# Softmax denominators in four column tiles, and one addition moved behind two maxima

## What is computed

```python
q = (layernorm(x) @ Wq).reshape(B, Nq, h, dh)        # 1 x 2048 x 16 x 64
k = (context @ Wk).reshape(B, Nk, h, dh)             # 1 x 1601 x 16 x 64
v = (context @ Wv).reshape(B, Nk, h, dh)
scores = einsum('bqhd,bkhd->bhqk', q, k) * scale
attn = softmax(scores, axis=-1)                      # exp(s - max) / sum
out = einsum('bhqk,bkhd->bqhd', attn, v) @ Wo + bo
x = x + out                                          # then the experts
```

## Time and profile before

| | us |
|---|---|
| median of three runs | 1381.43 |
| the profiled execution | 1375.65 |
| its span, first to last instruction | 1373.9 |
| TensorE matmuls busy | 1296.3 (94%) |
| VectorE busy | 1023.0 (74%) |
| GpSimd busy | 906.8 (66%) |
| ScalarE busy | 798.8 (58%) |

### The profile page before, as it was taken

The page is one execution under the profiler, slowest core; times in us unless marked ns, Lnnn a source line. Parts: engine busy times, 40 slices in busy tenths (PEclk is TensorE's granted clock), DMA queues, the critical chain, the costliest instruction groups (busy, mean ns, idle before and its releaser), DMA issues. The chain is left out here.

```text
span 1373.9 us, 24841 instructions
## 1 busy us (share of the span) xinstructions
PE 1296.3 (94%) x8308; PEld 819.1 (60%) x8308; DVE 1023.0 (74%) x1708; ACT 798.8 (58%) x1061; POOL 906.8 (66%) x464
## 2 busy tenths in 40 slices
PE   7989999999999999999999999999999926999996
PEld 5655555555555555554555555555447915999996
DVE  5867877887787788778778877887977775666662
ACT  5456666666665666566566666656664213657753
POOL 3347877887787688779777877977687002445553
PEclk9999999999999999999999999999999956999998
DMA  9530010002001100200010010002313442545422
GB/s 275 201 111 9 25 42 31 17 20 62 17 25 39 37 17 16 65 17 17 26 57 16 17 57 25 17 17 77 128 39 123 160 151 60 146 130 126 106 37 28
DMA packets 76631, 88.83 MB, mean 65 GB/s; under 512 B 11579, under 2 KB 56412, under 8 KB 76508
## 3 DMA queue, kind: packets, MB, share of 16 engines
q1 hardware_dynamic: 69724, 78.32, 17.5%
q0 software_dynamic: 6784, 8.94, 4.0%
HBM read 58.98 MB, written 27.99 MB: 63 GB/s over the span
## 5 line engine op out<-in xcount | busy, mean ns | idle before, releaser
L915 POOL TENSOR_TENSOR acc_p<-acc_p,x_in 128x1024 f32<-128x1024 f32 x192 | 488.0, 2542 | 135.5 <-ACT x_in L1012 128.7
L112 DVE TENSOR_REDUCE mx_part<-ps_m 128x1 f32<-128x512 f32 x552 | 363.0, 685 | 173.5 <-PE ps_m L81 172.7
L1012 ACT ACTIVATE x_in<-ps_s 128x1024 f32<-128x1024 f32 x384 | 380.6, 1024 | 100.7 <-PE ps_s L831 71.3
L843 PE MATMUL ps_o<-x_in,v 128*64 128x512 f32 x1664 | 406.2, 606 | 0.0
L820 PE MATMUL ps_s<-q,k 64*128 64x512 f32 x2496 | 386.4, 396 | 1.2 <-ACT x_in L1012 1.2
L820 PEld LDWEIGHTS ps_s<-q,k 64*128 64x128 f32 x2496 | 273.8, 185 | 41.5 <-ACT x_in L1012 7.8
L81 PE MATMUL ps_m<-k,q 64*128 64x512 f32 x736 | 215.6, 456 | 9.8 <-PEq L228 3.8
L843 PEld LDWEIGHTS ps_o<-x_in,v 128*64 128x64 f32 x1664 | 99.5, 136 | 180.7 <-issue 140.7
L81 PEld LDWEIGHTS ps_m<-k,q 64*128 64x128 f32 x736 | 100.9, 184 | 168.3 <-issue 112.5
L915 DVE TENSOR_TENSOR acc_d<-acc_d,x_in 128x1024 f32<-128x1024 f32 x96 | 166.4, 1733 | 5.2 <-ACT x_in L1012 4.9
L697 ACT ACTIVATE kept<-ps_m 128x512 f32<-128x512 f32 x184 | 109.7, 596 | 83.0 <-PE ps_m L81 82.9
(11 more groups left out here) (251 smaller groups left out, 1936.3 us busy)
## 6 DMA issues: line engine op xcount, KB each, us to landing
w_in<-in_w SPq DMA_DIRECT2D x16, 1024.0 KB, 5.7
v_st<-rec_scr SPq DMA_DIRECT2D x64, 128.0 KB, 2.9
o_scr<-v_st SPq DMA_DIRECT2D x32, 256.0 KB, 2.1
v<-v_scr SPq DMA_DIRECT2D x8, 832.0 KB, 5.2
v_scr<-c_in SPq DMA_DIRECT2D x10, 512.0 KB, 3.9
c<-o_scr SPq DMA_DIRECT2D x2, 1792.0 KB, 8.0
x_in<-in_x SPq DMA_DIRECT2D x4, 512.0 KB, 9.8
m_rows<-mx_t SPq DMA_DIRECT2D x128, 1.0 KB
```

The source lines that it names most:

```text
L112: dve.tensor_reduce(part[:, j // S.MF, j % S.MF:j % S.MF + 1], bank[:, 0:S.MC], AX.X, ALU.max).then_inc(done or G.rough_used[hd], 1)
L843: last = pe.matmul(ps_o[hd * HP:hd * HP + DH, :], v[b][:, s, hd * DH:(hd + 1) * DH], probs[:, g % RING, hd * QC:(hd + 1) * QC], start=(s = ...
L915: eng.tensor_tensor(acc, other, probs[:, (u * KT + t) % RING, :], ALU.add).then_inc(done, 1)
L1012: act.activation(probs[:, g % RING, :], ps_s[:, g % 2, :], ACT.Exp, bias=G.pad_bias[:, 0:1] if s == KT - 1 else 0.0, scale=SCALE).then_inc ...
```

## The change

The denominators are computed in four column tiles instead of two: each matmul takes 32 columns of ones and 256 columns of sums and writes 32 partitions. ScalarE copies 256 columns instead of 512, and one DMA moves the four rows in place of two that move a row each. In VectorE's order the addition of tiles 2 and 3 stands behind the two maxima of slot 4.

```diff
+DEN_TILES = 4
...
+    DP, DQ = P // DEN_TILES, UQ // DEN_TILES
...
         def pe_den(pe, u, unit, bank=None):
             pe.wait_ge(joined, unit + 1)
-            for b in range(2):
-                last = pe.matmul((ps_x if bank is None else bank)[b * HP:(b + 1) * HP, :], G.ones[:, 0:HP], acc_p[:, u % 2, b * QC:(b + 1) * QC],
-                                 start=True, stop=True)
+            for i in range(DEN_TILES):
+                last = pe.matmul((ps_x if bank is None else bank)[i * DP:(i + 1) * DP, 0:DQ], G.ones[:, 0:DP],
+                                 acc_p[:, u % 2, i * DQ:(i + 1) * DQ], start=True, stop=True)
             last.then_inc(den_ready, 1)
...
-            wait_for(act, den_moved, 32 * unit)
-            act.activation(den_sb[:], (ps_x if bank is None else bank)[:], ACT.Copy).then_inc(den_copied, 1)
+            wait_for(act, den_moved, 16 * unit)
+            act.activation(den_sb[:], (ps_x if bank is None else bank)[:, 0:DQ], ACT.Copy).then_inc(den_copied, 1)
...
             sp.wait_ge(den_copied, unit + 1)
-            for b in range(2):
-                sp.dma_start(den_c[8 * b:8 * b + 8, :], den_sb[b * HP:b * HP + 1, :]).then_inc(den_moved, 16)
+            sp.dma_start(den_c[:], den_sb[0:P:DP, :]).then_inc(den_moved, 16)
...
-            dve.wait_ge(den_moved, 32 * (unit + 1))
+            dve.wait_ge(den_moved, 16 * (unit + 1))
...
                 if s == MAX_SLOT and not (last and u == UNITS - 1):
                     dve_max(dve, unit + 1)
-                if s == DVE_TILES[1] + 1:
-                    add_tile(dve, 0, u, unit, slot - s, dve=True)
                 if job:
                     j, ahead = job
                     dve_rough(dve, j, unit + ahead, (unit + ahead) * MJOBS + j)
+                if s == DVE_TILES[1] + 1:
+                    add_tile(dve, 0, u, unit, slot - s, dve=True)
...
-            G.den_sb = lasting("den_sb", [P, S.QC], F32)
+            G.den_sb = lasting("den_sb", [P, S.UQ // DEN_TILES], F32)
```

## The result

The changed kernel took 1403.90 us, the median of four runs (1401.84 to 1406.14), against 1381.40 us for the kernel before: 1.0157 times as long, with a 95% interval of 1.0144 to 1.0170. That is 22.5 us slower. The profiled execution took 1406.14 us.

The account below looks back on a forecast made before the run. TensorE was taken to bound the attention loop. 21 x 1.42 = +29.8, 7 x 0.66 = +4.6 and 3 x -0.27 = -0.8 gave +33.6 us on 1381.43: 1415.0 us, range 1398 to 1425.

Parts of the forecast that it names:

- GpSimd stands first by 0.27 us in 21 units: Attention loop: GpSimd's addition of tile 4 starts at 541.17, VectorE's moved addition only at 541.44, in 21 units.
- VectorE is kept out for the whole instruction, about 3.2 us: VectorE's addition of tiles 2 and 3 ends 1.08 us after GpSimd's; mean about 3.2 us instead of 1.22.
- VectorE is not kept out: Rival: VectorE's addition isn't blocked or comes first everywhere; 31 x -0.27 = -8.4, 1373.0 us; chance 0.11.
- The maximum of slot 5 comes 1.42 us later and TensorE waits for it: Slot 5's first maximum moves from 543.13 to 544.55; TensorE's load for slot 6's rough scores moves to 545.30.
- The unit pays all of it, +1.42: Each of 21 units lengthens by the whole shift, +1.42 us; together +29.8 us.
- nothing behind the wait has slack: TensorE bounds the attention loop, so whatever it is made to wait is lost, with nothing given back.
- My lower bound: A stalled unit costs at least +1.2 us, if a waited-for load hands over to its matmul 0.2 us faster.
- The third units are a tie, counted +0.66: Seven third units of a pair: additions tie; +1.60 us if GpSimd is first, -0.27 if VectorE; mean +0.66, sum +4.6.
- Part one saves 0.27 us where it is seen: Denominators in four column tiles on TensorE take 0.69 us against 0.96, form changes included; saves 0.27 us a unit.
- Last pair 3 x -0.27 = -0.8: Last head pair, three units: VectorE has no projection to finish, is in time, and the tiles' gain shows.
- The small edits are worth nothing: ScalarE's shorter copy of the denominators and one DMA instead of two change nothing TensorE waits for: 0.
- A sign that missed: TensorE waits for VectorE's maxima some 1.7 us in each of 21 to 28 units, 35 to 47 us in all.

Follow-up runs that it names:

- order alone: Kernel before with VectorE's addition of tiles 2 and 3 moved behind slot 4's two maxima, still two column tiles: 1409.80 us, ratio 1.0170.
- tiles alone: Changed kernel with VectorE's addition of tiles 2 and 3 put back ahead of the maxima, four column tiles kept: 1387.63 us, ratio 1.0013.
- GpSimd held, two tiles: Kernel before with VectorE's addition behind the maxima, and GpSimd's addition of tile 4 waiting for it: 1379.55 us, ratio 0.9986.
- GpSimd held, four tiles: Changed kernel with GpSimd's addition of tile 4 waiting until VectorE's addition of tiles 2 and 3 is done: 1377.67 us, ratio 0.9941.
- GpSimd's addition in two: Changed kernel with GpSimd's addition of tile 4 done as two instructions of 512 columns: 1386.24 us, ratio 1.0003.
- addition between the maxima: Changed kernel with VectorE's addition of tiles 2 and 3 placed between slot 4's two maxima: 1384.13 us, ratio 1.0023.
- more matmuls, same form: Kernel before with each denominator matmul cut into two of 256 columns, in the same two column tiles: 1382.04 us, ratio 1.0006.

## Why the prediction was right, step by step

I forecast +33.6 us and 1415.0; it came to +22.5 and 1403.9. The mechanism is the forecast one, in the forecast units; two terms were too large, one is missing, and one that I put at nothing is not nothing in the third units.

- **GpSimd stands first by 0.27 us in 21 units.** Right: 0.26 in the unit shown, and the periods name the same 21.
- **VectorE is kept out for the whole instruction, about 3.2 us.** Right: 3.19 at the median. The experiments that turn GpSimd's place round, and cut its instruction in two, show it as the cause; the two that undo one part each put all of the loss on the order. The rival "VectorE is not kept out" falls. The Trainium skill (SBUF — State Buffer, SBUF: two separate sides) has the rule that fits: VectorE with two inputs in SBUF and a GpSimd operation that reads SBUF exclude each other for a whole instruction, and the one that starts first wins. All rows here agree with it, the halves above all. The section of the Trainium skill that I weighed for the rival (Advanced Engine Details and Errata, VectorE Performance Modes) names only two-port instructions of VectorE; the 3.19 us decides.
- **The maximum of slot 5 comes 1.42 us later and TensorE waits for it.** Right to 0.01: from the values matmuls to that maximum it is 558.55 - 553.87 = 4.68 us after and 543.13 - 539.87 = 3.26 before. The rough load moves by 5.42 - 4.01 = 1.41.
- **The unit pays all of it, +1.42.** Too large: +1.19. I had two bounds, 1.2 and 1.42, and took the upper. From the waiting load to the next values it is 559.94 - 559.29 = 0.65 us. For before I take the rough load at 543.88 and the values that follow it, at 544.78 in the lines below, the timeline of TensorE in the unit of the earlier trace rows: 0.90.

```profile
544.09 0.39 PE L81 MATMUL ps_m<-k,q 64*128 64x512 f32 x1
...
544.78 1.08 PE L843 MATMUL ps_o<-x_in,v 128*64 128x512 f32 x4
```

  So 0.25 of the 1.41 is given back, and the step of mine that failed is that nothing behind the wait has slack. Most of it lies in the handing over: in the stream the matmul of this load came 0.21 us behind it (543.88, 544.09), after the wait the two start together (559.29). My lower bound said just this, and I set it aside. Over 21 units this is 21 x 0.23 = 4.8 us of the 11.1 that I was off.
- **The third units are a tie, counted +0.66.** The tie was right in size and wrong in its end. The two starts are equal within 13 ns in the records of all seven, and VectorE won every time, in the kernel with the order alone too. That is the case I had priced at -0.27; it brought -0.44. 7 x (0.66 + 0.44) = 7.7 us of the miss.

  What it brought beyond the 0.28 of the tiles comes by way of ScalarE. Here are the timelines of TensorE, ScalarE and TensorE's loads for a third unit, before and then after:

```profile
511.52 1.03 PE L857 MATMUL ps_x<-acc_p,ones 128*64 128x512 f32 x4
514.68 0.65 PE L843 MATMUL ps_o<-x_in,v 128*64 128x512 f32 x2
...
513.61 0.59 ACT L697 ACTIVATE kept<-ps_m 128x512 f32<-128x512 f32 x1
...
514.25 0.18 PEld L81 LDWEIGHTS ps_m<-k,q 64*128 64x128 f32 x1
...
526.06 0.64 PE L859 MATMUL ps_x<-acc_p,ones 128*32 128x256 f32 x8
528.68 0.65 PE L845 MATMUL ps_o<-x_in,v 128*64 128x512 f32 x2
...
527.57 0.59 ACT L699 ACTIVATE kept<-ps_m 128x512 f32<-128x512 f32 x1
...
528.21 0.18 PEld L81 LDWEIGHTS ps_m<-k,q 64*128 64x128 f32 x1
```

  The load of the slot's last rough scores goes out 0.05 us after ScalarE's copy of a bank to `kept`, in both kernels. That copy stands in ScalarE's queue behind the copy of the denominators. It ends 2.68 us after the denominators' start before and 2.10 after the change, and the values follow 0.54 us earlier (3.16 and 2.62), where the denominators alone give 0.39 (0.96 and 0.57). No kernel changes the copy alone, so this is read from the traces and not shown by an experiment. The kernel that holds GpSimd back has these times too, and loses its 0.16 later in the unit, where VectorE's addition of tile 7 is late.
- **Part one saves 0.27 us where it is seen.** Right in the sum: from the values matmuls to the rough load it is 556.31 - 553.87 = 2.44 us after and 542.60 - 539.87 = 2.73 before, so 0.29, and 0.28 by the 18 units of the two kernels with GpSimd held back. Its terms: the four tiles with their exit take 0.57, and the way in from 64-column tiles costs 0.10 (554.78 to 555.74 is 0.96, where two pairs without a change of form take 0.86), together 0.67 where I had 0.69. The Trainium skill (TensorEngine Tiling (Array Packing), Key Properties) says that a change of mode drains the array; the 0.10 us on the way in agrees with it, and without such a price I would have forecast 0.43.
- **Last pair 3 x -0.27 = -0.8.** Right as far as it is seen: the two periods that the loop shows are -0.47 and -0.27; the third ends outside the loop.
- **The small edits are worth nothing.** Right in the stalled units, where the terms above leave nothing for them. Not in the third units: ScalarE's copy takes 0.38 instead of 0.60 us there as everywhere, and behind it stands the copy that TensorE does wait for. The earlier trace rows are of a unit in which it doesn't.
- **Missing: the loop's back edges**, +2.8 us in the profiled execution.
- **A sign that missed.** I had said that TensorE would wait some 1.7 us in each such unit, 35 to 47 us in all. TensorE's matmuls wait 1.31 us in each and 30.9 in all; the 1.7 is seen on its loads, which sit idle 1.76 us in the unit shown.

By measured terms the units give 25.0 - 3.1 - 0.7 = +21.2, with the back edges up to +24.0; the medians give +22.5. That the low end of my forecast was +22.5 too is chance: it takes the third units at -0.27 instead of -0.44 and has no back edges. One more thing was missed without harm: that in most units the tiles alone would gain nothing, since the second maximum of slot 4 was already as late as the denominators.

## What to carry to other kernels

Before an instruction of VectorE that reads two SBUF operands is moved by a few tenths of a microsecond, look at what GpSimd starts in the same stretch: the price isn't the shift but the rest of the other engine's whole instruction, and the cure may be a semaphore that sets who goes first (here from +1.6% to -0.6%). The engine that is made to wait then runs late, and may shut the other out at a later step, as it did here in the third units. When a stream waits, cost the wait by the shift less what the piled-up work behind it runs faster, and take a gain at a place only after asking which second wait ends there.

## What the runs showed that I had not expected

**Who wins a near tie.** In the third units the records of the two additions start within 13 ns of each other, GpSimd's mostly first, and VectorE won all seven. There GpSimd's step ahead of it ended 32 to 41 ns after VectorE's start (525.68 and 525.65 in the unit shown). In the kernel before there are seven cases, 138.12 in the earlier trace rows among them, where GpSimd's previous step ended 7 to 18 ns after VectorE's start; there GpSimd's next step, recorded 25 to 31 ns ahead of VectorE, won. So the start of a GpSimd record that follows another back to back is not its moment of getting in. Where the edge lies, between an end of 18 and of 32 ns after VectorE's start, was not tried.

**The gap at the loop's back edge.** TensorE's first instruction of a loop iteration has a gap for which no engine is named. The loop's body has 64 more records on TensorE with four matmuls of denominators a unit (eight more records of loads and matmuls in each of eight units), and the first gap grows from 1.05-1.08 us to 1.80-2.18. The second is clearly longer in only three of these six kernels (1.64 to 1.89 us, against 1.32 to 1.45). Three kernels, TensorE's matmul behind the first gap: before, after, and the kernel with more matmuls of the old form.

```profile
439.16 0.61 PE L81 MATMUL ps_m<-k,q 64*128 64x512 f32 x2 [1.08 <-issue]
```

```profile
449.50 0.67 PE L81 MATMUL ps_m<-k,q 64*128 64x512 f32 x2 [1.87 <-issue]
```

```profile
438.77 0.63 PE L81 MATMUL ps_m<-k,q 64*128 64x512 f32 x2 [2.18 <-issue]
```

**The clock behind it.** In the changed kernel the granted clock fell to 0.50, the level of 1.2 GHz, some 1.3 us behind the end of this gap and for some 3 us, with TensorE busy all the time. The busy times of one microsecond there (columns as in the earlier trace rows) and the eight values records in it, which take 3.44 us instead of 1.94:

```profile
451.00:452.00 1.00, 1.00 (x4) 0.29 (x4) 1.00 (x2) 0.73 (x1) 0.00 (x0) 0.50 0.10 33
...
451.16 3.44 PE L845 MATMUL ps_o<-x_in,v 128*64 128x512 f32 x8
```

In the kernel with more matmuls, behind a longer gap, it did not fall:

```profile
440.00:441.00 1.00, 1.00 (x8) 0.34 (x6) 1.00 (x2) 0.61 (x1) 0.00 (x0) 1.00 0.06 14
...
440.27 1.94 PE L843 MATMUL ps_o<-x_in,v 128*64 128x512 f32 x8
```

| kernel | first gap, us | second gap, us | granted clock of 0.50 behind |
|---|---|---|---|
| before | 1.08 | 1.43 | neither |
| order alone | 1.08 | 1.32 | neither |
| GpSimd held, two tiles | 1.05 | 1.45 | neither |
| after | 1.87 | 1.89 | first |
| tiles alone | 1.80 | 1.79 | second |
| GpSimd held, four tiles | 2.01 | 1.64 | first |
| GpSimd's addition in two | 1.83 | 1.42 | first |
| addition between the maxima | 1.98 | 1.41 | neither |
| more matmuls, same form | 2.18 | 1.47 | neither |

Four of the eight gaps of 1.79 us and more were followed by the low clock, and none of the ten shorter ones. Each such fall costs some 1.5 us, and each kernel was profiled once, so what decides between the gaps of 1.79 to 2.18 us stays open. So does what makes the first gap grow: the trace names no releaser for it. My prediction had charged a wait of 1.43 us no loss of clock, which held for the waits of 1.31 us in the stalled units: from 120 to 1020 us the granted clock of the changed kernel is 1.00 everywhere but at that one place.
